# Second attention: the transpose of a pair's row maxima moves from the pair's last step into the next pair's first step, between its scores and its key projection

## The reference

```python
q = (queries @ wq_w + wq_b).reshape(B, S, H, DK).transpose(0, 2, 1, 3)
k_ext = jnp.concatenate([keys @ wk_w + wk_b, jnp.broadcast_to(mk, (B, MEM, H * DK))], axis=1)
v_ext = jnp.concatenate([values @ wv_w + wv_b, jnp.broadcast_to(mv, (B, MEM, H * DV))], axis=1)
...
scores = jnp.einsum('bhsd,bhtd->bhst', q, k) / jnp.sqrt(jnp.float32(DK))
attn = jax.nn.softmax(scores, axis=-1)
out = jnp.einsum('bhst,bhtd->bhsd', attn, v)
out = out.transpose(0, 2, 1, 3).reshape(B, S, H * DV)
return out @ wo_w + wo_b
```

## Time and profile before

| | |
|---|---|
| median of three runs | 1690.82 us (1685.74, 1690.82, 1690.84) |
| the profiled execution, its own time | 1692.89 us |
| its span in the trace | 1691.2 us |
| busy PE, PEld | 87%, 50% of the span |
| busy DVE, ACT, POOL | 52%, 29%, 27% |
| granted PE clock over the span | 0.929 of full speed |
| transposes of maxima (L1630) | 32 |

### The profile page before, as it was taken

One profiled execution on the slowest core, in us unless ns is written; L12 is line 12 of the kernel. 1 busy time (PEld: TensorE's weight loads), 2 busy tenths in 40 slices (PEclk: granted clock), 3 DMA queues, 4 the chain that ended last, 5 costly groups with the idle time before them and its releaser, 6 DMA issues. The chain is left out here.

```text
span 1691.2 us, 19036 instructions
## 1 busy us (share of the span) xinstructions
PE 1465.2 (87%) x6061; PEld 841.0 (50%) x6088; DVE 877.6 (52%) x1676; ACT 494.5 (29%) x618; POOL 450.9 (27%) x257
## 2 busy tenths in 40 slices
PE   5999898999628988993799999999999999977885
PEld 2334343343527777771344445444544454435774
DVE  5666667755520000014457565766476646636666
ACT  2443333435102222220133332333233323320221
POOL 2000000000231000004045353445354534552333
PEclk8999999999658999996699999999999999987998
DMA  6521213220355454506555553555455554302001
GB/s 158 141 38 31 38 19 50 38 38 1 131 209 142 175 170 156 196 22 135 86 75 88 75 75 52 80 85 76 59 75 87 75 75 69 45 0 103 1 1 50
DMA packets 63294, 136.15 MB, mean 81 GB/s; under 512 B 11648, under 2 KB 22272, under 8 KB 58624
## 3 DMA queue, kind: packets, MB, share of 16 engines
q1 hardware_dynamic: 60496, 127.26, 37.7%
q0 software_dynamic: 2736, 8.13, 1.4%
HBM read 58.55 MB, written 12.06 MB: 42 GB/s over the span
## 5 line engine op out<-in xcount | busy, mean ns | idle before, releaser
L1080 POOL TENSOR_TENSOR a_probs<-a_probs 128x1024 f32<-128x1024 f32 x128 | 304.1, 2375 | 397.1 <-PE a_p_mo L1659 396.6
L1151 ACT ACTIVATE a_probs<-a_p_s 128x1024 f32<-128x1024 f32 x160 | 163.8, 1024 | 340.2 <-PE a_p_s L1645 340.2
L424 DVE CUSTOM_DVE_ANT_0 a_scratch<-a_p_m,a_bias_q 128x512 bf16<-128x512 f32 x256 | 163.1, 686 | 84.1 <-PE a_p_m L579 84.0
L1366 DVE TENSOR_REDUCE a_max_ctx<-a_p_mo 128x1 f32<-128x512 f32 x256 | 161.5, 684 | 75.5 <-PE a_p_mo L1616 75.5
L334 ACT ACTIVATE a_probs<-a_p_s 128x1024 f32<-128x1024 f32 x128 | 130.5, 1024 | 143.4 <-PE a_p_s L604 138.6
L579 PE MATMUL a_p_m<-a_k_stack,a_q_stack 127*128 127x512 f32 x256 | 128.3, 544 | 14.6 <-DVE a_mx L424 7.0
L1659 PE MATMUL a_p_mo<-a_probs,a_v 128*64 128x512 f32 x512 | 138.7, 620 | 0.0
L1532 PE MATMUL a_p_s<-a_o_raw,a_w 128*128 128x256 f32 x480 | 123.6, 392 | 13.8 <-DVE a_o_raw L1296 13.8
L1644 PE MATMUL a_p_s<-a_q_hh,a_k_hl 128*128 128x512 f32 x256 | 130.2, 509 | 0.0
L1301 DVE TENSOR_TENSOR a_yb<-a_p_mo,a_yb 128x512 f32<-128x512 f32 x15 | 10.4, 692 | 218.6 <-PE a_p_mo L1541 218.6
L602 PE MATMUL a_p_s<-a_q_stack,a_k_stack 128*128 128x512 f32 x256 | 117.6, 487 | 2.9 <-DMA a_q_stack<-a_neg_max 2.9
(11 more groups left out here) (200 smaller groups left out, 2079.0 us busy)
## 6 DMA issues: line engine op xcount, KB each, us to landing
a_w<-in_L_w SPq DMA_DIRECT2D x30, 1024.0 KB, 7.9
a_q_hh<-a_hi SPq DMA_DIRECT2D x64, 256.0 KB, 5.6
a_k_hl<-a_hi SPq DMA_DIRECT2D x64, 128.0 KB, 6.9
a_k_hl<-a_lo SPq DMA_DIRECT2D x64, 128.0 KB, 7.3
a_k_h<-a_hi SPq DMA_DIRECT2D x32, 256.0 KB, 8.7
a_q_lm<-a_lo SPq DMA_DIRECT2D x32, 256.0 KB, 7.0
a_ctx_t<-in_ctx_t SPq DMA_DIRECT2D x8, 512.0 KB, 6.0
a_q_stack<-a_hi SPq DMA_DIRECT2D x32, 128.0 KB, 3.9
```

Source lines behind the costliest of these rows:

```text
L424: dve.tensor_tensor_reduce(scratch[:, fill.n % M_BANKS, :], m, bias_q[:, i % NT, :], 1.0, -3.0e38, ALU.add, ALU.max, mx[:, i:i + 1]).then_ ...
L1080: pool.tensor_tensor(probs[:, kt], probs[:, kt - 1], probs[:, kt], ALU.add)\
L1151: act.activation(probs[:, kt, :, :], p_s[:, (KT1 * p + kt) % 2, :, :], ACT.Exp).then_inc(exp_done.sem, 1)
L1366: dve.tensor_reduce(max_ctx[:, NT * head + t:NT * head + t + 1], m, AX, ALU.max)\
```

## The change

In the table `turn` leaves the last step and goes into the first step, between the two scores and `key`; it is then the transpose for pair `p + 1` instead of `p + 2`. SP's copy of `neg_max` moves from behind the key's five copies to between the query's three and the key's five of the next pair. The counts of banks and readers follow.

```diff
-        STEPS = (("query", "score", "score", "key", "times_v"),
+        STEPS = (("query", "score", "score", "turn", "key", "times_v"),
...
-                 ("out", "score", "maximum", "maximum", "total", "score", "turn", "times_v"))
+                 ("out", "score", "maximum", "maximum", "total", "score", "times_v"))
...
+                if what == "turn" and p == 0 and not behind:
+                    continue
...
-        FIRST = NT + 1
+        FIRST, DVE_FIRST = NT + 2, NT + 1
...
-            def stack(b, p):
+            def stack(b, p, turned):
 
                 split_ready.wait(sp, b, 2 * p + 1)
                 stack_query(p, 0, stacked.sem)
+                if turned:
+                    bring_maxima(b, p - BRING + RANK - 1)
                 split_ready.wait(sp, b, 2 * p + 2)
                 stack_key(p, 1, stacked.sem)
...
-                        stack(b, p + BRING)
+                        stack(b, p + BRING, p or behind)
+                    elif p + RANK <= PAIRS:
+                        bring_maxima(b, p + RANK - 1)
...
-                    if ahead or p + RANK < PAIRS:
-                        bring_maxima(b, p + RANK)
...
-                                turn_maxima(b, fill, p + RANK)
+                                turn_maxima(b, fill, p + RANK - 1)
...
-                nm_ready.wait(pe, b, RANK)
                 if behind:
-                    banks = Banks(b, readers=((m_free, -1), (m_free, 0), (nm_ready, RANK)))
+                    banks = Banks(b, readers=((m_free, -2), (m_free, -1), (m_free, 0)))
                 else:
-                    banks = Banks(b, FIRST, FIRST, ((m_free, FIRST - 1), (m_free, FIRST), (nm_ready, RANK)))
+                    nm_ready.wait(pe, b, RANK)
+                    banks = Banks(b, FIRST, DVE_FIRST, ((m_free, DVE_FIRST - 1), (m_free, DVE_FIRST), (nm_ready, RANK)))
...
-                                turn_maxima(b, banks, p + RANK)
+                                turn_maxima(b, banks, p + RANK - 1)
```

More of the change, by code:

```diff
@@ L852, in steps @@
                     continue
+                if what == "turn" and p == 0 and not behind:
+                    continue
                 if not ahead and (what in ("query", "key") and p + BRING >= PAIRS
-                                  or what in ("maximum", "turn") and p + RANK >= PAIRS):
+                                  or what == "maximum" and p + RANK >= PAIRS
+                                  or what == "turn" and p + RANK > PAIRS):
                     continue
@@ L869, in mixture_attention1 @@
         PER = fills(FILLS)
-        FIRST = NT + 1
-        BASE, DVE_BASE = BEFORE - FIRST, DVE_BEFORE - FIRST
+        FIRST, DVE_FIRST = NT + 2, NT + 1
+        BASE, DVE_BASE = BEFORE - FIRST, DVE_BEFORE - DVE_FIRST
         assert PER % M_BANKS == 0
@@ L991, in bring_maxima, with turn @@
                   .then_inc(nm_in.sem, 16)
-            def turn(b, ahead):
+            def turn(b, ahead, behind):
                 for p in range(PAIRS):
                     if ahead or p + BRING < PAIRS:
-                        stack(b, p + BRING)
+                        stack(b, p + BRING, p or behind)
+                    elif p + RANK <= PAIRS:
+                        bring_maxima(b, p + RANK - 1)
                     if p == PAIRS - BRING - 1 and ahead:
@@ L1014, in _ @@
             sp.dma_start(wo, A["L1_wo"]).then_inc(wo_in, 16)
-            turn(0, True)
+            turn(0, True, False)
             with sp.Fori(1, B - 1) as b:
-                turn(b, True)
-            turn(B - 1, False)
+                turn(b, True, True)
+            turn(B - 1, False, True)
         @block.gpsimd
@@ L1404, in turn @@
                 fill = Fill(0 if behind else FIRST)
-                freed = 0 if behind else FIRST
+                freed = 0 if behind else DVE_FIRST
                 for p in range(PAIRS):
```

## The result

The changed kernel takes 1677.96 us (median of 8 runs, 1674.17 to 1683.53), the kernel before 1690.03 us in the same comparison (8 runs, 1684.57 to 1692.71). The ratio is 0.9935, with a 95% interval of 0.9914 to 0.9956. By this ratio it is 11.0 us less (7.4 to 14.5); the two medians are 12.1 us apart. A second comparison (6 runs against 11) gave 0.9931 [0.9910, 0.9952]. It is faster, as predicted, but by nearly twice the 6.3 us of the sum; 1677.96 lies under the range.

The account below looks back on a forecast made before the run. PE's instruction stream was taken to bound the kernel. The gains 2.7 + 2.0 - 0.5 + 2.1 = 6.3 us, put on the median of 1690.82, gave 1684.5 us, with a range of 1679.5 to 1689.5.

Parts of the forecast that it names:

- Part C: 26 ordinary boundaries between pairs: three PE distances fall from 0.81 to 0.73 us, 0.08 each, 2.1 us gained.
- rival 1: Pair 4 to pair 5: the lower clock behind the three waits goes too, 4.7 us more, 1679.8 us; chance 0.17.
- My lower end of 0.66: Ordinary boundary: lowest sum taken for the three distances, in us, against 0.81 before; 3.9 us of gain.
- Rival 2: Transpose before the key projection costs its full duration, 0.27 us; time 1688.0 us, or 1690.3 at the upper end; chance 0.24.
- Part B: Three query projections, pair 4 to 5: reciprocal 0.67 us earlier, 2.0 us gained less 0.5 for added transposes, net 1.5.
- Part A: First pair: the transpose's 1.00 us wait and the lower clock behind it go, 2.7 us gained.
- only the 1.0 us: First pair: gain left if the lower clock comes there in any case; kept for the range.
- What costs nothing: DVE's later negation, SP's earlier copy of neg_max and the bank waits: claimed to delay nothing, 0 us.
- rival 4: SP's moved copy makes the five key copies late, so ACT and PE wait; slower, 1699.0 us; chance 0.04.
- rival 3: Pair 4 to 5: something else holds the query projection as long as the reciprocal; 1686.5 us; chance 0.05.

Follow-up runs that it names:

- late-reciprocal kernel: Changed kernel plus one unused reduction on DVE ahead of each reciprocal, so that the reciprocal starts late; 1690.80 us.
- the kernel with neither wait nor jump: Changed kernel with the query projection no longer waiting for the reciprocal and DVE's loop over the middle batch items written out; 1665.01 us, ratio 0.9868.

## Why the prediction was wrong in size

**Part C is the step that failed first.** I took 0.08 us for an ordinary boundary, and it measured 0.20 (5.1 us instead of 2.1). With these 3.0 us more, the lower end of the range (1679.8, rival 1 in full) would have been 1676.8, and the measured 1677.96 within it. One term of the sum was mis-sized and one was missing. Transpose to key was 0.11, near my lower end of 0.10, and I took 0.15. Score to `times_v` and score to transpose were 0.32 and 0.24, within 0.01 of what I took. Missing was the key projection itself. I stopped at its start, and wrote only that it "waited a little for the reciprocal". In the kernel before its four matmuls take 1.84 to 1.92 us, afterwards 1.81, because the load of its first weights waited for the reciprocal (0.34 us in PEld's row of the kernel before); the vector engine's order alone gives that back. Of the 0.20 us the three distances make 0.15 and the key 0.05 in the first and last batch item, and 0.10 and 0.10 in the middle ones, where the key had waited more. The row was there to be read: the `times_v` behind the key. My lower end of 0.66 was right within 0.01, but 3.9 us is not the lower end of a sum that leaves a term out.

**Rival 2 is refuted.** The transpose costs the stream 0.11 us in front of a projection with 128 weight columns, not its duration of 0.27. The figure of about 275 ns that the Trainium skill gives (page "TensorE: Matmul & The Clock Gate", section "Part 4: PE-mode transpose") is the duration. The page doesn't say of what shape that kernel's transposes were; for the 128 x 8 one in fp32 here the trace agrees with it as a duration (0.27) and not as a cost. Whether the clock gate counts a transpose, no run here shows.

**Part B was right as a mechanism and too small by the clock.** The reciprocal starts right behind `mx`, the waits fell from 2.72 to 2.23 and 2.15, as I wrote ("about 2.2"). Without a lower clock on either side a boundary there falls from 8.89 (an unchanged one at full clock) to 8.24, 0.65 us or 1.9 in all, where I had 1.5: the reciprocal starts 0.74 us earlier behind `mx` instead of 0.67, and the transpose that is added costs 0.12 instead of 0.17. The other 3.3 us of the profile are two lower stretches less. I had this as rival 1, with 4.7 us for three stretches, less for one or two, and a chance of 0.17; for it I named the shorter wait. The runs don't bear out that a shorter wait stops it: behind waits of 2.13 to 2.24 us the lower clock came at 10 of 18 places of six executions, behind 1.99 to 2.01 at 2 of 3, behind 2.72 at 6 of 9, in the late-reciprocal kernel at 3 of 3. Of the 10, six are the first of the three places, where it came in all six executions, and four are among the twelve others. Whether a shorter wait makes it rarer, and why the first place is worse, stays open; these counts are too few. So two stretches less in the profile after were luck as far as these runs show.

**Part A was right in size, partly for a wrong reason.** The profile gave 2.8 us. But the lower clock behind the wait of 1.00 us came only in the profile of the kernel before; in the profiles of four other kernels with the same wait it did not. So 1.2 us are there each time and 1.6 come and go; I kept "only the 1.0 us" as an end and didn't see that one profile can't tell how often it applies.

**What costs nothing** was right for SP's copy; PE shows no wait for a bank at an ordinary boundary, and no ACT conversion waited for a copy, so rival 4 fell; rival 3 fell with part B. It was wrong for DVE. I looked for what is queued behind the negation, but not at what the order does at the loop's jump. Before, the jump was already paid for in part: both `a_lo` stood there behind it and started together at 1177.73, 3.29 us behind `o_norm` (the row names ACT's `a_hi`, but the first `a_hi` was done at 1174.46), and that pair took 15.82 us instead of 15.25. The rows of the kernel before:

```profile
1174.44 0.69 DVE L1392 TENSOR_TENSOR a_o_norm<-a_o_raw,a_recip 128x512 f32<-128x512 f32 x1
1177.73 1.41 DVE L1357 SCALAR_TENSOR_TENSOR a_lo<-a_p_mo,a_bqk,a_hi 128x512 fp32r<-128x512 f32 x2 [2.59 <-ACT a_hi L1141]
```

With the negation between the two, a second gap of 1.34 us follows the first of 2.50, and the pair takes 16.85. That is 1.0 us lost, 0.8 in the second profile.

**Sum without any clock:** 5.1 + 1.2 + 1.9 - 1.0 = 7.2 us. In the profile the kernel before has more of the lower stretches, 1.6 + 3.3 us, and the sum is then 12.1. The measured 11.0 (7.4 to 14.5) may contain some of them; how many came in the executions without a profile isn't known, and the interval takes in 12.1 and misses 7.2 by 0.2. With every term of the clock-free sum right and part A's clock as I took it, 1690.8 - 8.8 = 1682.0 us would have stood there; of what is left to 1677.96, the clock in part B is the likely part, but only the profile shows it.

## What to carry to other kernels

When an instruction moves, measure from a landmark before it to one behind everything that could have waited because of it, not from start to start of the neighbours: a bank that is read earlier also shortens the matmul group after it. A wait that a profile shows three times is better asked for its reason than shortened: here one count lower in it gave 12.8 us at its three boundaries, against 12.1 for the whole change, each in one trace (without the lower clock some 7.9 against 7.2). And a price that contains the lower clock must be split into the wait and the clock, since only the first comes back in each execution.

## What the hardware showed unexpectedly

The level of the clock behind a PE wait isn't decided by the wait's length alone: 1.00 us led to 0.51 once and to 1.00 four times, 1.25 and 1.22 us to a lower level where 1.02, 1.20 and 1.32 us at the same place did not, 2.72 us to both. Where it falls, some 1.5 us are lost each time. That alone doesn't explain the 8 to 11 us between executions of one kernel: up to 9.7 us can already lie before the attention's first query projection (818.5 to 828.2 us over the fourteen profiles), and the kernel with neither wait nor jump still varies from 1660.68 to 1667.54 us.

With the changed order DVE stood still for 2.4 to 2.5 us and again for 1.2 to 1.4 us behind its loop's jump back in five profiles, and for neither with the loop written out. In a sixth, of the kernel with the late reciprocal, it jumped back too and did not stand still. The Trainium skill, page "Runtime: NRT & Kernel Launch", section "Instruction fetch mechanics", says that a taken branch to instructions outside the two pages at hand has to fetch them before it goes on. The loop written out and the word "issue" fit this, but the trace names no fetch, and no run here shows why the one kernel was spared. That the cost came out only once the negation stood behind the jump was new to me: before, it was a slower pair among others, 0.57 us over its kind.
